# Three maps of a fused kernel in one unrolled stage, on adapters that arrive contraction first in quarters of their output columns

## The reference, cut to what matters

```python
x = x + einsum('bct,bcd->bdt', x, W0[cond])          # W0 is (16, 32, 32): mixes the 32 rows of a batch
x = x + einsum('bsi,boi->bso', x, W1[cond])          # W1 is (16, 512, 512): an adapter of each batch
x = x + einsum('bct,bcd->bdt', x, W2[subj]) + b2.T   # W2 is (32, 32, 32), b2 (32, 1, 32)
x = x + attention(x, Wq, Wk, Wv, Wo, k_cache, v_cache, ...)
```

## Time and profile before

| what | us |
|---|---|
| median of three runs | 2431.99 (2431.39 to 2432.40) |
| the profiled execution's own time | 2430.95 |
| its span | 2429.2 |
| `stage_prep` | 0 to 54.4 |
| `stage_maps` | 54.4 to 184.4 |
| `stage_values` | from 184.4 |

### The profile page before, as it was taken

One profiled execution on the slowest core, in us unless ns is written; L12 is line 12 of the kernel. 1 busy time (PEld: TensorE's weight loads), 2 busy tenths in 40 slices (PEclk: granted clock), 3 DMA queues, 4 the chain that ended last, 5 costly groups with the idle time before them and its releaser, 6 DMA issues. The chain is left out here.

```text
span 2429.2 us, 50595 instructions
## 1 busy us (share of the span) xinstructions
PE 2318.3 (95%) x14977; PEld 1934.9 (80%) x14977; DVE 1790.6 (74%) x3412; ACT 1344.7 (55%) x2635; POOL 1145.5 (47%) x1330
## 2 busy tenths in 40 slices
PE   6997899999999499999999999999999998899999
PEld 5335777777777399999999999999999997788887
DVE  4565189999999588888888888888888886522221
ACT  6563388888887355555555555555555554421111
POOL 0320044444444376777776777777777675000000
PEclk9998999999999699999999999999999999999999
DMA  9335323333332688888888888888888885843441
GB/s 313 99 102 177 103 66 108 109 109 108 108 104 79 196 280 298 289 280 290 297 289 290 277 291 288 297 294 281 285 292 296 286 292 172 256 133 96 129 138 60
DMA packets 463993, 501.42 MB, mean 206 GB/s; under 512 B 102069, under 2 KB 396981, under 8 KB 457654
## 3 DMA queue, kind: packets, MB, share of 16 engines
q1 hardware_dynamic: 427062, 366.37, 47.6%
q0 software_dynamic: 36864, 134.23, 15.8%
HBM read 404.02 MB, written 96.47 MB: 206 GB/s over the span
## 5 line engine op out<-in xcount | busy, mean ns | idle before, releaser
L1092 POOL TENSOR_TENSOR att_probs<-att_probs,att_inverse 128x512 f32<-128x512 f32 x512 | 535.1, 1045 | 289.1 <-DVE att_inverse L1288 284.5
L1196 ACT ACTIVATE att_probs<-att_probs,att_low 128x544 f32<-128x544 f32 x512 | 383.9, 750 | 515.8 <-DVE att_low L1275 454.7
L1153 PE MATMUL att_o<-att_probs_t,att_values 128*128 128x128 f32 x4096 | 540.9, 275 | 0.0
L1275 DVE CUSTOM_DVE_ANT_0 att_probs<-att_score,att_mask,att_batch_cols 128x544 f32<-128x544 f32 x512 | 399.9, 781 | 138.3 <-PE att_score L1118 99.6
L1153 PEld LDWEIGHTS att_o<-att_probs_t,att_values 128*128 128x128 f32 x4096 | 497.6, 192 | 0.0
L1284 DVE COPY att_probs_t<-att_turn 128x512 f32<-128x512 f32 x512 | 350.8, 685 | 1.2 <-PE att_turn L1133 1.2
L1078 POOL DMA_INDIRECT att_values<-L_cond_v_cache,att_v_rows_of x256 | 283.7, 1108 | 82.4 <-POOL att_v_rows_of L1074 49.7
L1118 PE MATMUL att_score<-att_keys_raw,att_queries_raw 128*128 128x288 f32 (+1 forms) x1024 | 290.7, 407 | 29.0 <-DMA att_queries_raw<-q_t 26.8
L1133 PE MATMUL att_turn<-ident,att_probs 128*128 128x128 f32 x2048 | 311.1, 274 | 1.2 <-POOL att_probs L1092 0.9
L787 PE MATMUL proj_proj<-x3t_hi,proj_w_hi 128*128 128x512 f32 x640 | 266.7, 417 | 6.9 <-DVE proj_w_lo L847 6.9
L1251 DVE TENSOR_TENSOR att_keys_lo<-att_keys_raw,att_keys_hi 128x384 fp32r<-128x384 f32 (+1 forms) x320 | 259.8, 812 | 17.6 <-ACT att_keys_hi L1189 17.6
(11 more groups left out here) (132 smaller groups left out, 4008.6 us busy)
## 6 DMA issues: line engine op xcount, KB each, us to landing
att_keys_raw<-L_cond_k_cache SPq DMA_DIRECT2D x1024, 128.0 KB
q_t<-proj_q_out SPq DMA_DIRECT2D x32, 1024.0 KB, 3.9
att_queries_raw<-q_t SPq DMA_DIRECT2D x64, 512.0 KB
o_t<-att_heads_out SPq DMA_DIRECT2D x64, 512.0 KB
out_o_raw<-o_t SPq DMA_DIRECT2D x32, 1024.0 KB, 5.8
prep_natural<-L_cond_weight SPq DMA_DIRECT2D x16, 1024.0 KB, 8.4
w_nat<-L_cond_Wq SPq DMA_DIRECT2D x8, 1024.0 KB, 5.4
v_new<-values_v_out SPq DMA_DIRECT2D x64, 128.0 KB, 2.0
```

The source lines that it names most:

```text
L1092: nc.gpsimd.tensor_tensor(probs[:, k, 0:L], probs[:, k, 0:L], inverse[:, k:k + 1].to_broadcast([P, L]), ALU.mult).then_inc(probs_ready, 1)
L1153: last = nc.tensor.matmul(o, values[j][:, t, h * D:(h + 1) * D], probs_t[m % 2][:, t * P:(t + 1) * P], start=(t == 0), stop=False, skip_gr ...
L1196: nc.scalar.activation(probs[:, k, :], probs[:, k, :], ACT.Exp, bias=low[k][:, 0:1], scale=-1.0, accum_out=total[k][:, 0:1]).then_inc(exp_ ...
L1275: nc.vector.tensor_tensor_reduce(out=probs[:, k, :], in0=score_ps[:, LEFT:LEFT + KEYS], in1=mask[j][:], scale=batch_cols[j][:, h:h + 1], s ...
```

## The change

`stage_prep` and `stage_maps` go; `stage_front` takes their place, without a loop. The host hands the adapters over as (quarter of the output columns, contraction partition, adapter, contraction block, output column), so that PE transposes none of them; the tables come repeated for the four batches of a group. A unit is one quarter of the output columns (128) of one quad of groups (512 rows, 16 batches): 16 units, quarter by quarter. Two quarters of all adapters fit (4 MB each, in four DMAs); the third and fourth are loaded when the units of the first and second have been copied. The residuals of layers 0 to 2 are ones that DVE and POOL add to the diagonals of the tables and adapters, so that no residual is added to the results. Layer 0 is done for pairs of groups with `x` as the stationary operand, which gives the transposed result. The fills of a unit's 16 slots are split: 8 by DVE, 6 by ACT, 2 by POOL. The numbers are clamped once by DVE, and the registers are loaded with no check of their bounds.

```diff
+def stage_front(nc, x, weight1, cond, subj, w0, w2, bias2, wv, ident, w_nat, x3_dram, x3t_dram):
...
+    BY_ACT = ((1, 2, 3), (4, 5, 6))
+    BY_DVE = ((4, 5, 6, 7), (0, 1, 2, 3))
     with ExitStack() as ctx:
...
+        slots = [a_.sb(f"slots{h}", [P, HB, IC, P]) for h in range(2)]
+        x2 = [a_.sb(f"x2_{v}", [P, 4, P]) for v in range(2)]
...
+        def fill(copy, done, ids, k, h, batches):
+            for a, b in zip(ids, batches):
+                copy(slots[h][:, b].rearrange("p c o -> p (c o)"),
+                     adapters[k // QUADS % 2][:, bass.ds(a, 1)].rearrange("p a c o -> p (a c o)")).then_inc(done, 1)
...
+        def may_fill(engine, k, h):
+            if k % QUADS == 0 and h == 0:
+                engine.wait_ge(ones_added, (k // QUADS + 1) * CH)
+            if k:
+                engine.wait_ge(l1_halves, (k - 1) * 2 + h + 1)
...
+            def load_adapters(q):
+                if q >= 2:
+                    sp.wait_ge(slots_by_dve, (q - 1) * QUADS * 8)
+                    sp.wait_ge(slots_by_act, (q - 1) * QUADS * 6)
+                    sp.wait_ge(slots_by_pool, (q - 1) * QUADS * 2)
+                for j in range(CH):
+                    sp.dma_start(adapters[q % 2][:, j * CA:(j + 1) * CA].rearrange("p a c o -> p (a c o)"),
+                                 weight1[q, :, j * CA:(j + 1) * CA].rearrange("p a c o -> p (a c o)")).then_inc(adapters_loaded[q % 2][j], 16)
...
+            def store(k):
+                q, Q = divmod(k, QUADS)
+                rows = slice(Q * QR, (Q + 1) * QR)
+                sp.wait_ge(x3_kept, k + 1)
+                sp.dma_start(x3_dram[rows].rearrange("(g p) t -> p g t", p=P)[:, :, q * P:(q + 1) * P], x3[k % 2][:]).then_inc(x3_stored[k % 2], 16)
+                sp.wait_ge(x3t_kept, k + 1)
+                sp.dma_start(x3t_dram[:, q, rows], x3t[k % 2][:]).then_inc(x3t_stored[k % 2], 16)
+            sp.dma_start(cond_sb[:], cond.rearrange("(o b) -> o b", o=1)).then_inc(ids_loaded, 16)
+            sp.dma_start(subj_sb[:], subj.rearrange("(o b) -> o b", o=1)).then_inc(ids_loaded, 16)
...
+                load_x(p)
+            load_adapters(0)
+            sp.dma_start(w2_all.rearrange("p n d -> p (n d)"), w2).then_inc(w2_loaded, 16)
+            sp.dma_start(bias_all[:], bias2).then_inc(w2_loaded, 16)
+            for p in range(2, XR):
+                load_x(p)
+            load_adapters(1)
+            for p in range(XR, PAIRS):
+                load_x(p)
+            for k in range(UNITS):
+                store(k)
+                if k == 2:
+                    load_adapters(2)
+                if k == 4:
+                    load_wv(sp, wv, w_nat, slice(0, WV_EARLY), wv_loaded)
+                if k == 6:
+                    load_adapters(3)
+            for v in range(2):
+                sp.wait_ge(x3_stored[v], 16 * (UNITS // 2))
+                sp.wait_ge(x3t_stored[v], 16 * (UNITS // 2))
+            sp.wait_ge(wv_loaded, 16)
...
+            def maps2(Q):
+                subs = numbers(subj_sb, mybir.EngineType.Pool, Q * QB, QB, SUBJ)
+                for g in range(4):
+                    for b in range(GB):
+                        last = nc.gpsimd.tensor_tensor(diag2[:, Q * 4 + g, b * S:(b + 1) * S],
+                                                       w2_all[:, bass.ds(subs[g * GB + b], 1), :].rearrange("p n d -> p (n d)"),
+                                                       quadrant[:, b:b + 1].to_broadcast([P, S]), ALU.mult)
+                    last.then_inc(diag2_ready, 1)
+            def add_ones(q):
+                for j in range(CH):
+                    pool.wait_ge(adapters_loaded[q % 2][j], 16 * (q // 2) + 16)
+                    part = adapters[q % 2][:, j * CA:(j + 1) * CA, q, :]
+                    nc.gpsimd.tensor_tensor(part, part, ident[:].unsqueeze(1).to_broadcast([P, CA, P]), ALU.add).then_inc(ones_added, 1)
...
+            add_ones(0)
+            fills(0)
+            pool.wait_ge(w2_ready, 2)
+            maps2(0)
+            for k in range(UNITS):
+                if k + 1 < UNITS:
+                    fills(k + 1)
+                if k + 1 < QUADS:
+                    maps2(k + 1)
+                if k % QUADS == 2 and k // QUADS + 1 < IC:
+                    add_ones(k // QUADS + 1)
...
+            def maps0(Q):
+                ids = numbers(cond_sb, mybir.EngineType.DVE, Q * QB, QB, CONDS)
+                for g in range(4):
+                    for b in range(GB):
+                        rows = slice(b * S, (b + 1) * S)
+                        last = copy(diag0[rows, Q * 4 + g, b * S:(b + 1) * S],
+                                    w0_all[rows, bass.ds(ids[g * GB + b], 1), :].rearrange("p n d -> p (n d)"))
+                    last.then_inc(diag0_ready, 1)
+            def biases(Q):
+                subs = numbers(subj_sb, mybir.EngineType.DVE, Q * QB, QB, SUBJ)
+                for g in range(4):
+                    for b in range(GB):
+                        rows = slice(b * S, (b + 1) * S)
+                        last = copy(bias[rows, Q * 4 + g:Q * 4 + g + 1], bias_all[rows, bass.ds(subs[g * GB + b], 1)])
+                last.then_inc(bias_ready, 1)
...
+            def add_bias(k):
+                Q = k % QUADS
+                dve.wait_ge(l2_done, k + 1)
+                if k >= 2:
+                    dve.wait_ge(x3_turned, k - 1)
+                    dve.wait_ge(x3_stored[k % 2], 16 * (k // 2))
+                if k < QUADS:
+                    dve.wait_ge(bias_ready, Q + 1)
+                nc.vector.tensor_tensor(x3[k % 2][:], l2_ps[k % 2].rearrange("p (g o) -> p g o", g=4),
+                                        bias[:, Q * 4:(Q + 1) * 4].unsqueeze(2).to_broadcast([P, 4, P]), ALU.add).then_inc(x3_kept, 1)
...
+            maps0(0)
+            for p in range(2):
+                keep_x1(p)
+            for Q in range(1, QUADS):
+                maps0(Q)
+            fills(0)
+            nc.vector.tensor_reduce(quadrant[:], ident.rearrange("p (b c) -> p b c", b=GB), mybir.AxisListType.X, ALU.add).then_inc(w2_ready, 1)
+            dve.wait_ge(w2_loaded, 32)
+            nc.vector.tensor_tensor(w2_all[:], w2_all[:], eye[:].unsqueeze(1).to_broadcast([P, SUBJ, S]), ALU.add).then_inc(w2_ready, 1)
+            for Q in range(QUADS):
+                biases(Q)
+            for k in range(UNITS):
+                if k + 1 < UNITS:
+                    fills(k + 1)
+                if k + 1 < QUADS:
+                    for p in range(2 * k + 2, 2 * k + 4):
+                        keep_x1(p)
+                if k:
+                    add_bias(k - 1)
+            add_bias(UNITS - 1)
...
+            fills(0)
+            for k in range(UNITS):
+                if k + 1 < UNITS:
+                    fills(k + 1)
+                if k + 1 < QUADS:
+                    for p in range(2 * k + 2, 2 * k + 4):
+                        keep_x1(p)
+                keep_x2(k)
+                if k >= 2:
+                    keep_x3t(k - 2)
...
+            def layer0(p):
+                pe.wait_ge(x_loaded[p % XR], 16 * (p // XR) + 16)
+                pe.wait_ge(diag0_ready, 2 * p + 2)
+                for n in range(2):
+                    if p:
+                        pe.wait_ge(x1_kept[n], p)
+                    for c in range(2 * n, 2 * n + 2):
+                        for g in range(2):
+                            at = (c % 2) * 2 * P + g * P
+                            last = nc.tensor.matmul(x1_ps[n][:, at:at + P], xin[p % XR][:, g, c * P:(c + 1) * P], diag0[:, 2 * p + g, :],
+                                                    start=True, stop=True)
+                    last.then_inc(x1_done[n], 1)
+            def layer1(k):
+                Q = k % QUADS
+                if k >= 2:
+                    pe.wait_ge(x2_kept, k - 1)
+                for h in range(2):
+                    if k < QUADS:
+                        for n in range(2):
+                            pe.wait_ge(x1_kept[n], 2 * Q + h + 1)
+                    pe.wait_ge(slots_by_dve, (2 * k + h + 1) * 4)
+                    pe.wait_ge(slots_by_act, (2 * k + h + 1) * 3)
+                    pe.wait_ge(slots_by_pool, 2 * k + h + 1)
+                    for g in range(2 * h, 2 * h + 2):
+                        for c in range(IC):
+                            for b in range(GB):
+                                at = (Q * 4 + g) * P + b * S
+                                last = nc.tensor.matmul(l1_ps[k % 2][b * S:(b + 1) * S, g * P:(g + 1) * P], x1t[:, c, at:at + S],
+                                                        slots[h][:, (g % 2) * GB + b, c, :], start=(c == 0), stop=(c == IC - 1))
+                    last.then_inc(l1_halves, 1)
...
+                for g in range(4):
+                    last = nc.tensor.matmul(l2_ps[k % 2][:, g * P:(g + 1) * P], diag2[:, 4 * Q + g, :], x2[k % 2][:, g, :],
+                                            start=True, stop=True)
...
+                layer1(k)
```

(42 more changed lines are left out.)

417 lines of the change are left out of this document (120 added, 297 removed).

## The result

The changed kernel takes 2405.92 us (median of 4 runs, 2404.29 to 2406.31), the kernel before 2431.69 us (2430.72 to 2432.4) on the same chip: ratio 0.9893, 95% interval 0.9876 to 0.991. The forecast was 2402, with a range of 2386 to 2428. The profiled execution took 2405.73 us, span 2403.6.

The account below looks back on a forecast made before the run. PE was taken as the bound from unit 4, DVE then POOL before it: 82.0 + 58.3 + 3.6 + 4 = 147.9, then 4.0 and 3.1 to 155.0 us; -30.4 on 2431.99 gives 2402 us, range 2386 to 2428.

Parts of the forecast that it names:

- Layer 1's rate: Layer 1 on PE: 32 rounds of four matmuls at 0.11 us each, 3.6 us a unit with the start.
- issue-bound rival: Layer 1 on PE: issuing a matmul costs 0.12 us, 15.4 us a unit, 2573 us in all; chance 0.05.
- eleven periods: Units 4 to 15: PE is the bound, 5.3 us a unit, 58.3 us for eleven.
- Fills: Slot fills: 0.34 us each on DVE, 0.53 on ACT, 0.8 on POOL; as bound from unit 4, 2415, chance 0.15.
- POOL's ones: POOL's residual ones on a quarter's adapters: 4 products at 1.4 us, the first late set over at 80.1 us.
- The first layer 1: PE begins layer 1 of unit 0 at 28.3 us, behind DVE's register loads, small copies and fills.
- The start as a whole: Units 0 to 3: DVE's lots, then POOL's work, set the pace; layer 1 of unit 4 starts at 82.0 us.
- The changes of a quarter: At units 8 and 12, POOL's ones and late adapters delay PE by 2 us each, between 0 and 5: 4 us.
- The end: After the last layer 1, at 147.9 us: 4.0 us of remaining work and 3.1 to the next stage.
- first landing: Start of the front: numbers, w0 and the first x land by 4.2 us.
- The first rival's second price: Layer 1 at about 62 ns per matmul: 7.9 us a unit, the kernel some 25 to 40 us slower than before.
- If anything behind 184.4 us changes in length: Sign against the forecast: any stage after the front changing in length by more than a few us.

Follow-up runs that it names:

- e4: The changed kernel with POOL adding ones to one column in 128 only in quarters 1 to 3: 2400.98 us, ratio 0.9876.
- e1: The changed kernel with four buffers instead of two for the stores (x3 and x3t): 2410.16 us, ratio 0.9916.
- e2: The changed kernel with the adapters of quarters 2 and 3 asked for two units earlier and wv later: 2401.72 us, ratio 0.9883.
- e6: The changed kernel with DVE's four lots of biases moved from ahead of unit 1 into the loop: 2393.08 us, ratio 0.9841.
- e12: e6 with the late adapters asked for one megabyte at a time, behind the stores of successive units: 2404.23 us, ratio 0.9887.
- e13: e12 with each late quarter's megabytes asked for sooner, two of them behind one store: 2394.83 us, ratio 0.9849.
- e8: The changed kernel without the adapter loads of quarters 2 and 3, older data used again: 2394.42 us, ratio 0.9851.
- e3: The changed kernel with the edits of e1 and e2 together: 2407.19 us, ratio 0.9905.
- e11: The edits of e6 and e7 in one kernel: 2390.99 us, ratio 0.9833.
- e7: e3 with four waits, met long before, added to DVE's front so its program is as long as in the changed kernel: 2401.55 us, ratio 0.988.
- e5: The changed kernel with the run-time bounds checks of the register loads kept: 2452.11 us, ratio 1.0084.

## Why the prediction was right, point by point

- **Layer 1's rate: right.** 0.11 us a round and 3.6 us a unit, against 0.116 and 3.70. The issue-bound rival is out at both of its prices (15.4 and 7.9 us a unit): 128 matmuls, each with its load, in 3.70 us are 0.029 us each. A unit is 5.16 for 5.3, since layer 2 and the transposes overlap; over eleven periods that is -1.5 us.
- **Fills: right in kind.** One takes 0.35 us on DVE in the start (2.77 for eight) and 0.45 in the warm units (3.60), 0.57 on ACT (3.42 for six), 0.88 on POOL, for 0.34, 0.53 and 0.8. In a warm unit they were never the bound; in units 7 and 11, where POOL's ones stood beside them, they were.
- **The first layer 1: right, by errors that cancel.** 28.9 for 28.3. The register load was 1.1 to 1.35 us, not 2.2, the small copy 0.19 to 0.20 us apart, not 0.144: a lot of 16 is 3.0, not 2.3. I had the two exposed one after the other; they overlap. That alone would have made the three later lots over 3 us shorter than my 13.5, but they took 12.9, since POOL's ones held four of the copies for 2.9 us in sum, which I hadn't thought of. The two pairs of layer 0 took 4.8 for 2.7, and the last register load, 1.5, was hidden.
- **The start as a whole: 5.5 us too dear.** Biases over at 43.2 for 46.8, layer 1 of unit 1 at 50.6 for 54.5, POOL's ones over at 74.0 for 80.1, unit 4 at 76.5 for 82.0. POOL's 16 diagonals took 3.2 to 3.5 us, with most of their register load beside earlier work, where I had 5.5.
- **POOL's ones: right in kind.** 1.26 to 1.46 us a product, 5.0 for four, near the 1.41 chosen rather than 1.05. They set unit 4 (e4: 6.3 to 5.2). The price was given for one side only: I had DVE slow POOL's products, and not POOL's products hold DVE's copies (0.41 us alone, 1.50 beside one).
- **The changes of a quarter: the step that failed.** "These delays lie beside each other; I take 2 us each": 4 us. From the starts of units 7, 8, 9 and 11, 12, 13 the excess over 5.16 is 5.9 + 1.5 and 5.7 + 1.2, together 14.4, so 10.4 us too little, and past my own upper end of 5 each.

  The first half of the sentence held: the two changes take 34.8 us without POOL's long products (e4), 26.1 without the transfers (e8), and 35.0 with both. The sizes did not. I had 10.8 us for the 4 MB; their last megabyte took 15.8 us from the first issue. So the transfers end last: the last megabyte and POOL's ones behind it hold the fills (ACT 7.3 us), and the store queued behind the adapters holds DVE's add (5.4). These two end together, at 100.5 and 100.8 us, and four buffers for the stores (e1) took off only 1.2 us of front.

  Two terms I had at nothing. POOL's ones hold DVE's fills while layer 1 of units 7 and 11 needs them: 4.68 us in place of 3.63, 2.1 in both, and 3.9 with the short products of e4. And the gap leaves PE at a lower clock: the layer 1 behind it takes 5.20 us, not 3.70, at a granted clock of 0.70 (the levels are 0.5 and 1.0, so part of it at 1.2 GHz), 2.7 us in both changes. The other 9.6 of the 14.4 us are the waits. The row of that layer 1:

```profile
103.05:108.25 5.20, 5.20 (x129) 5.00 (x129) 3.41 (x9) 3.33 (x7) 0.88 (x1) 0.70 0.41 124
```

  Without the loads 26.1 - 4 x 5.16 = 5.5 us are left, more than what I had said for everything.

  PE's own stops under "issue" were in no term either, up to 3.0 us each (e4), and they come and go with the adapters' transfers (there in the changed kernel, e2, e6, e12 and e13, gone in e8). In the changed kernel there is one, 1.5 us in the first late change, and it cost nothing: PE would have waited for DVE's add, over at 100.8, all the same. The second late change has none and is as long. They are part of what e2 paid and most of what e13 did (6.4 us in sum). That PE's instructions are late there fits the packets (behind e13 above), which go through the same 16 DMA engines as the loads; no run changed the instruction stream alone, and how the loads hold a packet back is not shown.
- **The end:** 8.0 us from the last layer 1 to the next stage, for 7.1.
- **The sum:** -5.5 (start) - 1.5 (period) + 10.4 (changes) + 0.9 (end) = +4.3: 159.3 for 155.0. The total is 3.9 us above the forecast. The time came out close by luck: two errors of opposite sign, 7.0 us too dear and 11.3 too cheap, stood against each other.
- **Slips in the prediction's sums:** the first landing is given as 4.2 us with terms that add to more (0.8 + 2.2 + 3.4), so the 2.2 is not in it (`w0` was there at 4.2), and three sums are 0.2 us off (9.2, 46.8 and 82.0 where the terms give 9.4, 46.6 and 81.8). The first rival's second price, 7.9 us a unit against 3.6, comes to 21 us above the kernel before if 12 units pay it and 38 if all do, not 25 to 40. None matters for the result.
- **"If anything behind 184.4 us changes in length":** not in the changed kernel, but in e1 and e3, by 7 us, and for a reason that the prediction had not among its rivals.

The kernels e6 and e11 beat both: 2393 and 2391 us, -1.6 and -1.7% of before. The start was the larger reserve: the biases alone, moved by a few lines, gave 12.8 us, half of what the whole change had given.

## What to carry to other kernels

When a load is laid beside unrolled products, price what queues behind it: stores whose buffers someone waits for, the last piece of the load itself (from issue to landing, not its share of a burst), and the instruction stream; 4 MB cost about 4.5 us here (8.9 for the two late loads, e8). Ahead of the first products, put into an in-order engine's queue only what those products need (the biases were needed one unit later). Where GpSimd and VectorE work at the same time, price what each does to the other: here a VectorE copy of 0.41 us took 1.50 beside a GpSimd product. And compare all stages after an edit in one: here four waits fewer in VectorE's first stage cost 7 us in its third.

## What the runs showed of the hardware that was not expected

- A DVE copy that meets one of POOL's products lasts about as long as the product: 1.50 us in place of 0.41 for 128x512 (product 1.45), 1.27 and 1.16 us in place of 0.17 for 32x32 (product 1.26). Beside POOL's own copies of 0.88 us it takes 0.83.
- Four instructions more or less in VectorE's program decide whether it stops for 8.5 us at the first turn of a loop some 450 us later (e3 and e7), with packets on the instruction queue under it.
- All 14 of PE's stops of over 1 us that wait for nothing shown end 1.3 to 1.5 us after a 16 KB packet of the instruction queue.
- The adapters in rows of 8 KB moved at 418 GB/s from 22 to 26 us, against 388 GB/s in the earlier trace rows with rows of 2 KB at about the same DMA share (1.01 and 1.05; one stretch of each, and no run changed the row length alone):

```profile
22.00:26.00 4.00, 0.00 (x0) 0.00 (x0) 3.35 (x20) 0.23 (x1) 0.00 (x0) 0.50 1.01 418
```

- One megabyte of them lands 2.5 us behind the one before in the start's burst and 2.5 to 3.9 us in the late ones, but takes a median of 7.3 us from issue to landing when asked for alone beside the stores (e12, third quarter).
- A checked register costs VectorE 0.18 us for a FUSED_REGOPS and 0.02 for the assert, some 0.3 us in all: DVE idles 4.7 to 5.1 us ahead of a lot of 16 where it had idled 0.3 to 0.6, and the checks of a lot stand ahead of its copies (e5).
